# Turning attention probabilities, q and k on VectorE and through DRAM instead of on TensorE, in a single-core attention and FFN kernel

## The reference

```
xn = layernorm(x)
q = xn @ Wq.T   (32 heads of 128)      k, v = xn @ Wk.T, xn @ Wv.T   (8 heads of 128)
q, k = rmsnorm(q, q_norm_w), rmsnorm(k, k_norm_w)     (per head)
scores = q @ k.T / sqrt(128) + slope[head] * (key - query), causal; 4 query heads share one k, v head
attn = softmax(scores);  out = attn @ v;  s = out @ Wo.T
ffn(xn) = (silu(xn @ w_gate.T) * (xn @ w_up.T)) @ w_down.T     (inner width 1376)
result = x + s * silu(ffn(xn))
```

## Time and profile before

| | |
|---|---|
| time of 3 runs, median | 2454.05 us (2453.86 to 2455.95) |
| profiled execution, its own time | 2455.46 us |
| its span, first to last instruction | 2453.7 us |
| busy: PE, PEld, DVE, ACT, POOL | 2422.6, 2070.7, 1693.7, 1236.1, 756.9 us |
| granted TensorE clock, mean | 0.998 |
| DMA traffic | 92.19 MB in 23289 packets, mean 38 GB/s |

### The profile page before, as it was taken

One profiled execution on the slowest core, in us unless ns is written; L12 is line 12 of the kernel. 1 busy time (PEld: TensorE's weight loads), 2 busy tenths in 40 slices (PEclk: granted clock), 3 DMA queues, 4 the chain that ended last, 5 costly groups with the idle time before them and its releaser, 6 DMA issues.

```text
span 2453.7 us, 37432 instructions
## 1 busy us (share of the span) xinstructions
PE 2422.6 (99%) x13232; PEld 2070.7 (84%) x13232; DVE 1693.7 (69%) x3788; ACT 1236.1 (50%) x2548; POOL 756.9 (31%) x2053
## 2 busy tenths in 40 slices
PE   7999999999999999999999999999999999999998
PEld 6888888888888888878888888888888888888887
DVE  7777777777778787823377787777777777777132
ACT  4555554555545555543355555555555545545333
POOL 2323231413233323244522232323232314131443
PEclk9999999999999999999999999999999999999999
DMA  3010000000000000023320101010000000010232
GB/s 130 1 40 4 27 18 27 18 27 18 27 18 27 18 27 18 27 91 125 112 78 1 44 1 44 1 44 1 27 18 26 18 27 18 1 44 14 90 103 103
DMA packets 23289, 92.19 MB, mean 38 GB/s; under 512 B 6592, under 2 KB 6720, under 8 KB 19136
## 3 DMA queue, kind: packets, MB, share of 16 engines
q1 hardware_dynamic: 23104, 89.80, 10.5%
HBM read 85.60 MB, written 4.19 MB: 37 GB/s over the span
## 4 chain that ended last, share of the span: by engine, by line
PE 96%; DVE 2%; ACT 1%; issue 1%; POOL 0%; DMA 0%; DVEq 0%; ACTq 0%; POOLq 0%
PE out_ps L401 17%; PE score_ps L377 16%; PE out_ps L414 14%; PE qkv_ps L351 14%; PE ring_ps L388 10%; PE qkv_ps L352 7%; PE score_ps L504 5%; PE qkv_ps L504 4%; PE ring_ps L520 4%; PE ring_ps L359 2%; PE out_ps L520 1%; PE ring_ps L364 1%; PE score_ps L351 0%; DVE y L997 0%; DVE xT_lo L868 0%
## 5 line engine op out<-in xcount | busy, mean ns | idle before, releaser
L597 ACT ACTIVATE pT_hi<-ring_ps 128x512 fp32r<-128x512 f32 x576 | 344.0, 599 | 509.8 <-PE ring_ps L388 497.2
L818 DVE TENSOR_TENSOR pT_lo<-ring_ps,pT_hi 128x512 fp32r<-128x512 f32 x576 | 396.8, 690 | 90.6 <-ACT pT_hi L597 86.0
L589 ACT ACTIVATE probs<-probs,low_min 128x896 f32<-128x896 f32 (+7 forms) x512 | 395.2, 774 | 50.4 <-DVE low_min L810 50.1
L1016 POOL TENSOR_SCALAR rs_x<-sq_sum 128x5 f32<-128x5 f32 x122 | 24.8, 203 | 1128.1 <-DVE sq_sum L749 1128.1
L388 PE MATMUL ring_ps<-ident,probs 128*128 128x128 f32 x2304 | 345.6, 273 | 0.0
L388 PEld LDWEIGHTS ring_ps<-ident,probs 128*128 128x128 f32 x2304 | 281.7, 140 | 42.1
L810 DVE CUSTOM_DVE_ANT_0 probs<-score_ps,rel_sb,slope 128x512 f32<-128x512 f32 (+5 forms) x504 | 301.7, 599 | 5.7 <-PE score_ps L377 4.3
L377 PE MATMUL score_ps<-kv_hi,qT_hi 128*128 128x320 f32 (+4 forms) x760 | 275.6, 363 | 3.0 <-DVE xT_lo L868 2.0
L401 PE MATMUL out_ps<-pT_hi,kv_hi 128*128 128x512 f32 x576 | 265.8, 461 | 2.9 <-DVE pT_lo L818 2.6
L377 PE MATMUL score_ps<-kv_hi,qT_lo 128*128 128x320 f32 (+4 forms) x760 | 261.0, 343 | 0.0
L377 PE MATMUL score_ps<-kv_lo,qT_hi 128*128 128x320 f32 (+4 forms) x760 | 260.3, 342 | 0.0
(11 more groups left out here) (178 smaller groups left out, 5293.5 us busy)
## 6 DMA issues: line engine op xcount, KB each, us to landing
qkv_raw<-w_ffn_dram SPq DMA_DIRECT2D x44, 768.0 KB, 4.2
qkv_raw<-w_qkv_dram SPq DMA_DIRECT2D x15, 1536.0 KB, 6.9
o_raw<-w_o_dram SPq DMA_DIRECT2D x16, 1024.0 KB, 4.8
o_raw<-x_dram SPq DMA_DIRECT2D x4, 1024.0 KB, 6.7
out_dram<-y SPq DMA_DIRECT2D x16, 256.0 KB, 3.7
probs<-x_dram SPq DMA_DIRECT2D x3, 1024.0 KB, 7.9
qkv_raw<-w_qkv_dram SPq DMA_DIRECT2D x4, 384.0 KB, 6.6
probs<-x_dram SPq DMA_DIRECT2D x2, 512.0 KB, 4.8
```

The source lines that it names most:

```text
L589: act.activation(row, row, ACT.Exp, scale=-1.0, bias=low_min[:, i % 2, h, HEAD_CHUNKS[i] - 1:HEAD_CHUNKS[i]], accum_out=row_sum[:, i % 2, ...
L597: act.activation(pT_hi[:, n % SLOTS, :], ring_ps[:, ring_bank(r), :], ACT.Copy).then_inc(ring_high, 1)
L818: dve.tensor_tensor(out=pT_lo[:, n % SLOTS, :], in0=ring_ps[:, ring_bank(r), :], in1=pT_hi[:, n % SLOTS, :].bitcast(F32), op=ALU.subtract) ...
```

## The change

Probabilities are turned in two stages. VectorE transposes 32x32 blocks in place in `probs` (`turn_blocks`), and SP writes the tile to DRAM and reads it back so that the blocks land in their transposed places: one DMA out, and for each group of up to 4 chunks four DMAs back into `pT`, one for each 32 partitions. q and k of all but the first two tiles of a row go the same way (`scale_qk` with a transpose behind it, `turn_qk` on SP). The division by the row sums is gone from the probabilities; instead the four reciprocals of a tile go through DRAM (`rec_out_at`) and come back broadcast over partitions, and the weighed result is multiplied by them (`scale_att`). `weigh` of tile i - 1 stands as a block behind all scores of step i. `probs` is now one buffer, `pT` is new (two groups of 4 chunks), `pT_hi` keeps 4 slots, and `pT_lo` has 3. Scores have 3 banks instead of 2, and the projections have two pairs of banks. `sum_squares` is gone; ACT squares with an accumulated sum, in five instructions of 128 columns instead of one of 640. `low_att` moves from VectorE to GpSimd, and so do 7 of the 36 `low_probs` of a unit (POOL_LOWS).

The core of the diff follows: the functions of VectorE, the order of VectorE's step, SP, TensorE's step, ACT, GpSimd.

```diff
+                    return
+                dve.tensor_tensor(out=qk[i % 2].rearrange("p (b g n) -> p g b n", b=BLOCKS, g=G + 1),
+                                  in0=acc[:, 0:(G + 1) * P].rearrange("p (g b n) -> p g b n", b=BLOCKS, g=G + 1),
+                                  in1=rq[:, i % 2, :].unsqueeze(2).unsqueeze(3).to_broadcast([P, G + 1, BLOCKS, SQUARE]),
+                                  op=ALU.mult).then_inc(qk_done, 1)
+                dve.wait_ge(qk_done, t)
+                dve.transpose(qk[i % 2], qk[i % 2]).then_inc(qk_turned, 1)
...
+
+            def bias(U, i, k):
 
                 n = SCORE_AT[i] + k
                 h, part = k // HEAD_CHUNKS[i], k % HEAD_CHUNKS[i]
                 lo, hi = [(part + end) * CHUNK_WIDTH[i] for end in range(2)]
                 if k == 0 and i == 0:
...
+            def turn_blocks(U, i, h):
+
+                dve.wait_ge(exped, (tile(U, i) - 1) * G + h + 1)
+                row = by_head[:, h, 0:(i + 1) * BLOCKS, :]
+                dve.transpose(row, row).then_inc(probs_turned, 1)
+
+            def reciprocals(U, i):
+                t = tile(U, i)
+                dve.wait_ge(exped, t * G)
+                if t > 2:
+                    dve.wait_ge(rec_out, (t - 2) * 16)
+                dve.reciprocal(rec[:, i % 2, :], row_sum[:, i % 2, :]).then_inc(rec_done, 1)
+
             def low_probs(U, i, j):
-                r, n = RING_AT[i] + j, TURN_AT[i] + j
-                dve.wait_ge(ring_high, U * RING + r + 1)
-                dve.tensor_tensor(out=pT_lo[:, n % SLOTS, :], in0=ring_ps[:, ring_bank(r), :],
-                                  in1=pT_hi[:, n % SLOTS, :].bitcast(F32), op=ALU.subtract).then_inc(ring_lowd, 1)
-
-            def divide(U, i):
-
-                dve.wait_ge(exped, (U * TILES + i + 1) * G)
-                dve.reciprocal(rec[:, :], row_sum[:, i % 2, :]).then_inc(rec_done, 1)
-                dve.wait_ge(rec_done, U * TILES + i + 1)
-                for h in range(G):
-                    row = probs[i % 2][:, h, 0:(i + 1) * P]
-                    dve.tensor_scalar(row, row, rec[:, h:h + 1], None, ALU.mult).then_inc(divided, 1)
-
...
+            def scale_att(U, i):
+                t = U * TILES + i - 1
+                dve.wait_ge(weighed, (t - 1) // TILES * TURNS + TURN_AT[(t - 1) % TILES + 1])
+                dve.wait_ge(rec_back[t % 2], ((t - 1) // 2 + 1) * 16)
+                scaled = att[i % 2][:, :].rearrange("p (g a n) -> p g a n", g=G, a=BLOCKS)
+                dve.tensor_tensor(out=scaled, in0=out_ps[:, :].rearrange("p (a g n) -> p g a n", g=G, a=BLOCKS), in1=scaled,
+                                  op=ALU.mult).then_inc(att_scaled, 1)
 
             def add_y(U, i, copy):
...
+                    for k in range(sooner, chunks):
+                        bias(U, i, k)
+                        h, part = divmod(k, HEAD_CHUNKS[i])
+                        if k - sooner < len(sooner_lows):
+                            low_probs(V, p, sooner_lows[k - sooner])
+                        if part == HEAD_CHUNKS[i] - 1 and h >= 2:
+                            turn_blocks(U, i, h - 2)
+                    for j in sooner_lows[max(0, chunks - sooner):]:
+                        low_probs(V, p, j)
...
+                                low_x(0, t)
+                    if i < TILES:
+                        turn_blocks(U, i, G - 2)
+                        turn_blocks(U, i, G - 1)
+                        reciprocals(U, i)
+                    for j in lows:
+                        low_probs(V, p, j)
...
+                m, slot = turned_before(t), t % 2
+                alone(qk_turned, m + 1)
+                if m >= 2:
+                    alone(qk_back[m % 2], m // 2 * BLOCKS * 16)
+                sp.dma_start(qk_out_at[slot], qk[i % 2]).then_inc(qk_out, 16)
+                alone(qk_out, (m + 1) * 16)
+                there = qk_out_at[slot].rearrange("(a r) (b m) -> b r a m", a=BLOCKS, b=BLOCKS)
+                for k in range(BLOCKS):
+                    sp.dma_start(qk[i % 2][k * SQUARE:(k + 1) * SQUARE, :].rearrange("r (a m) -> r a m", a=BLOCKS),
+                                 there[k]).then_inc(qk_back[m % 2], 16)
...
+            def turn_probs(U, i):
+
+                t = tile(U, i)
+                slot = t % 2
+                alone(probs_turned, t * G)
...
+                sp.dma_start(turned_out[slot, 0:i + 1].rearrange("j p m -> p j m"), by_chunk[:, 0:i + 1, :]
+                             ).then_inc(probs_out, 16)
+                alone(rec_done, t)
+                if t > 2:
+                    alone(rec_back[slot], (t - 1) // 2 * 16)
+                sp.dma_start(rec_out_at[slot].rearrange("g p -> p g"), rec[:, i % 2, :], allow_slow_non_contiguous=True).then_inc(rec_out, 16)
+                alone(probs_out, t * 16)
+                for part in range(GROUPS_IN[i]):
+                    lo, hi = part * GROUP, min((part + 1) * GROUP, i + 1)
+                    group = U * GROUPS + GROUP_AT[i] + part
+                    if group >= 2:
+                        done = chunks_to_group(group - 2)
+                        alone(low_by_dve, done // TURNS * DVE_LOW_AT[TURNS] + DVE_LOW_AT[done % TURNS])
+                        alone(low_by_pool, done // TURNS * POOL_LOW_AT[TURNS] + POOL_LOW_AT[done % TURNS])
+                    there = turned_out[slot, lo:hi].rearrange("j (a r) (b m) -> b r (j a) m", a=BLOCKS, b=BLOCKS)
+                    for k in range(BLOCKS):
+                        at = group % 2 * GROUP
+                        sp.dma_start(pT[k * SQUARE:(k + 1) * SQUARE, at:at + hi - lo, :]
+                                     .rearrange("r j (a m) -> r (j a) m", a=BLOCKS), there[k]).then_inc(probs_back[group % 2], 16)
+                alone(rec_out, t * 16)
+                if t > 2:
+                    alone(att_split, t - 2)
+                sp.dma_start(att[i % 2][:, :], rec_out_at[slot:slot + 1].rearrange("a g p -> a (g p)").to_broadcast([P, G * P])
+                             ).then_inc(rec_back[slot], 16)
+
...
-                ring_free(U, r, first)
-                for h in range(G):
-                    if j == 0:
-                        pe.wait_ge(divided, (U * TILES + i - 1) * G + h + 1)
-                    tr = pe.transpose(ring_ps[:, ring_bank(r), h * P:(h + 1) * P],
-                                      probs[p % 2][:, h, j * P:(j + 1) * P], ident[:, :])
-                tr.then_inc(ring_full, 1)
-
-            def weigh(U, i, j, turns, first):
-
...
             def step(U, i, first, last):
-                ahead = not (last and i >= TILES - 1)
+                if not (last and i >= TILES - 2):
+                    project(U + (i + 2) // TILES, (i + 2) % TILES, first and i + 2 < TILES)
...
+                for k in range(sooner):
+                    scores(U, i, k, first)
+                if not (first and i < 2):
+                    out_project(U, i)
+                for k in range(sooner, chunks):
+                    scores(U, i, k, first)
...
+            def squares(U, i, first):
+                t, acc = tile(U, i), acc_of(i, first)
                 act.wait_ge(projected, t)
-                if not first:
-                    act.wait_ge(summed, t - 1)
-                act.activation(qk_sq, acc[:, 0:(G + 1) * P], ACT.Square).then_inc(squared, 1)
-
-            def stage_v(acc, i, t, early):
-                if not early:
-                    act.wait_ge(v_split, t - VBUFS)
-                act.activation(v_nat[:, i % VBUFS, :], acc[:, BANK + P:BANK + KV], ACT.Copy).then_inc(v_staged, 1)
-
...
-            def high_probs(U, i, j, first):
-                r, n = RING_AT[i] + j, TURN_AT[i] + j
-                act.wait_ge(ring_full, U * RING + r + 1)
-                if not (first and n < SLOTS):
-                    act.wait_ge(weighed, U * TURNS + n - SLOTS + 1)
-                act.activation(pT_hi[:, n % SLOTS, :], ring_ps[:, ring_bank(r), :], ACT.Copy).then_inc(ring_high, 1)
+            def high_probs(U, i, j):
...
+                group = U * GROUPS + GROUP_AT[i] + j // GROUP
+                act.wait_ge(probs_back[group % 2], (group // 2 + 1) * BLOCKS * 16)
+                if U * TURNS + n >= HIGH_SLOTS:
+                    act.wait_ge(weighed, U * TURNS + n - HIGH_SLOTS + 1)
...
+                    highs = [] if i > TILES or first and i == 0 else list(range(p + 1))
+                    if i == 0:
+                        for j in highs[:HIGH_SLOTS]:
+                            high_probs(V, p, j)
+                        highs = highs[HIGH_SLOTS:]
+                    if not (last and i >= TILES - 2):
+                        squares(U + (i + 2) // TILES, (i + 2) % TILES, first and i + 2 < TILES)
...
+                        high_o(U, 1, not first)
+                    if i:
+                        for j in highs[:HIGH_SLOTS]:
+                            high_probs(V, p, j)
+                        highs = highs[HIGH_SLOTS:]
+                    if i < TILES:
```

(15 more changed lines are left out.)

642 lines of the change are left out of this document (319 added, 323 removed).

## The result

The changed kernel takes 4060.89 us (median of 4 runs, 4054.24 to 4065.72) against 2455.0 us before: a ratio of 1.654 (95% interval 1.651 to 1.657). The forecast was 2950 us, with a range of 2560 to 3320. The direction was right; the size was missed by 1111 us, 8.7 us in each of 128 steps.

What follows compares the result with a forecast made beforehand. The kernel before was taken as bound by TensorE, the changed one by a loop through DRAM: eight steps make 158.8 us a unit, 16 units plus 409 us for start, FFN and row ends give 2950 us, range 2560 to 3320.

Steps and rivals of the forecast that it cites:

- unit: Stretch of eight steps from one load of the slopes to the next; forecast to last 158.8 us, 16 of them.
- R: Round trip of a tile's probabilities out to DRAM and back: 8.1 to 15.0 us for 2 to 8 chunks.
- V: VectorE's work in a step from first low part to last transpose: 4.6 to 10.9 us for tiles 2 to 7.
- the sentence on the reciprocals: The reciprocals' 4-byte packets on the DMA queue: 0 to 1.5 us a step, 0 to 190 us in all, taken as 0.
- The loop: Once a step, tile i's transposes wait for tile i-1's way back: R + 0.6 + V, 13.3 to 25.8 us; chance 50%.
- The signs that the prediction named for it: In the profile after, tile 7's store issue to its first group's landing takes 12 to 16 us.
- Its bounds 0.78 and 1.55: Lower and upper price in us of each 256 KB chunk on the way back; the middle, 1.16, was taken.
- The q and k trip: q and k through DRAM, issued early in a step, wanted over 10 us later; claimed hidden behind the loop.
- Rival 1: The round trip is hidden and only the second path binds: 130 us a unit, 2493 us; chance 12%.
- the second path: Low parts, weighing, projection, Wo, first score and bias, then V, one behind another; sets step 1, 15.7 us.
- Rival 3: TensorE's clock falls after idling, projection and Wo take 12.5 instead of 6.9 us: 3160 us; chance 20%.
- Rival 4: The DMA queue binds, if 512-byte packets cost three times large ones: 190 us a unit, 3450 us; chance 8%.

Runs made afterwards that it cites:

- experiment 5: The change with the reciprocals padded and turned on VectorE, leaving as 16 packets of 128 bytes instead of 512 of 4; 3192.39 us, ratio 1.300.
- experiment 8: As experiment 5, with next slopes loaded right behind tile 7's store and weights in quarters and halves behind the ways back; 3134.32 us, ratio 1.278.
- experiment 6: The kernel before, with single transfers added behind its last store, each waited for, to price them; the 512 packets of 4 bytes took 8.2 us.
- experiment 7: As experiment 5, but ACT does all exponentials ahead of the previous tile's high parts and VectorE all transposes ahead of low parts; 3182.37 us, ratio 1.296.
- experiment 4: The change with each DMA back reading packets of 2 KB instead of 512 bytes into 32 partitions, blocks left unturned; 3873.28 us, ratio 1.578.

## Why the prediction was wrong

**Where the 1111 us went.** 869 us are the 4-byte packets (experiment 5 against the change), 58 the loads at the turn of a unit (experiment 8), and 3134 - 2950 = 184 us are left. Of the last the unit shows the place. SP's issues of `turned_out<-probs` in experiment 8, the first and the last of nine from tile 7 to the next tile 7; the table has the distances from one to the next:

```profile
697.80 0.38 SPq L309 DMA_DIRECT2D turned_out<-probs  x1
...
867.02 0.38 SPq L309 DMA_DIRECT2D turned_out<-probs  x1
```

| step | 0 | 1 | 2 | 3 | 4 | 5 | 6 | 7 | unit |
|---|---|---|---|---|---|---|---|---|---|
| forecast | 19.9 | 15.7 | 13.3 | 16.6 | 20.4 | 23.0 | 24.1 | 25.8 | 158.8 |
| experiment 8 | 22.8 | 16.7 | 16.4 | 16.8 | 22.3 | 22.6 | 24.9 | 26.9 | 169.2 |

With the small packets gone, steps 3 and 5 to 7 are within 1.1 us of the forecast; steps 0, 2 and 4 are 2 to 3 us longer. The unit is 10.4 us longer, 16 x 10.4 = 166 of the 184 us. (The next unit is 167.6; there step 2 takes 14.5.)

None of it is the round trip. From the issue of the store to ACT's first high part it is 9.5, 11.9, 12.1, 13.6, 13.7 and 14.5 us for n = 3 to 8, where R was 10.0, 11.9, 12.7, 13.5, 14.3 and 15.0. Step 0 has SP's row in front of its store (experiment 8). Step 2 has GpSimd, by the chain of waits (start us, us, what):

```profile
737.66 2.34 POOL o_lo L1122
...
741.24 1.24 POOL attT_lo L1162
742.52 4.61 PE out_ps L493 x12
```

GpSimd splits the new Wo there, and `attT_lo` stands behind it; TensorE waits 2.89 us for it, and the projection by Wo then takes 4.6 us at a granted clock of 0.64, against 3.0 at 1.00 in the next unit. The forecast had called `low_att` on GpSimd hidden. In step 4 it is V: 9.4 us instead of 7.9, with one low part of 1.77 us where the others take 0.69 (GpSimd takes its own low part at that moment) and scores at a granted clock of 0.50.

**The step that failed** is the sentence on the reciprocals: "Between nothing and 1.5 us a step, 0 to 190 us in all; I take 0 because the queue is idle then." Measured, 8.2 us for the transfer alone, and 869/128 = 6.8 us a step. With this part mended the forecast's sum is 242 us short, and the kernel of experiment 5, at 3192 us, lies inside its range. Two things were wrong in the sentence. The upper end, 1.5 us, was a guess at 2 KB; the nearest row of the trace was that of a small load, and no row had more than one packet to a partition of such a size. I should have looked at the packets: 512 of 4 bytes in one DMA, of a kind that no row prices, so its upper bound is far away. And the reason, an idle queue, was wrong twice: in an idle queue the transfer takes 8.2 us all the same (experiment 6), and L311 is issued 0.6 us behind the store, so it never has an idle queue; it lands either with the store or ahead of the way back. The loop has no slack, so both come to the same. The Trainium skill would have helped: DMA: Bandwidth & Descriptors, in the part Measured of its section Bandwidth, puts the floor of a small transfer down to its packets, at about 10.5 ns each. By that 512 packets are 5.4 us, an estimate. The trace has 8.2 us to the landing, but not as time of the packets: their records end 1.3 us behind the issue. The page names another direction and another way of issue than here.

**R otherwise.** The round trip was right where it was priced: 6.9 us for a group back against 6.7, and 1.75 MB out in 6.7 against 7.2. The signs that the prediction named for it hold in experiment 8, with 14.5 us for tile 7 (12 to 16 expected). Its bounds 0.78 and 1.55 hold it; the middle was the right choice, as the nearest row alone was not.

**V and the transposes** were right within 0.3 us in the change's steps of tiles 5 and 6 and 3% in the price of a column; step 4 of experiment 8 is 1.5 us over.

**The q and k trip.** "Hidden" was right in the steps of large tiles and wrong in the small ones behind the turn of a unit: `qk_out_at<-natural` is 6% of the chain of the change. Weights of 1.5 MB stood ahead of it in the queue and the slopes behind 2 MB on their way back; with both moved, it still holds up the store of tile 0.

**Rival 1 and the second path.** The mechanism is real and the price was 326 us too low: the path goes through ACT (squares, the copy of v, the weights) and GpSimd (Wo, `attT_lo`), and not only through TensorE and VectorE. With the trip free a unit is still 151 us, against 169 with it, so the loop alone can give back 18 us a unit at the most. The order of experiment 7 opens the loop and lengthens the second path, and the two nearly cancel (10 us).

**Rival 3, the clock.** It fell as described: around one step of tile 5 the windows of the change read as follows (us, busy us of PE, PEld, DVE, ACT, POOL, then the granted clock, DMA share, GB/s).

```profile
1058.00:1066.00 8.00, 1.02 (x5) 0.47 (x3) 0.63 (x2) 0.41 (x1) 7.00 (x17) 0.79 0.58 107
...
1071.00:1075.00 4.00, 4.00 (x12) 3.30 (x12) 3.96 (x11) 2.55 (x5) 0.00 (x0) 0.50 0.33 82
...
1118.00:1124.00 6.00, 6.00 (x32) 5.10 (x31) 1.79 (x3) 1.57 (x11) 2.22 (x7) 1.00 0.14 21
```

TensorE had idled 10.59 us before 1070.65, and then ran at 0.50 of 2.4 GHz, which is the 1.2 GHz level. The rule of the Trainium skill cited in the prediction (TensorE: Matmul & The Clock Gate, Part 1: The HAM clock gate) agrees: an idle engine comes back at half rate. In that step this fell mostly on scores that VectorE paced. The last window is of the next step, and most of its projection lies there at the full level, where the rival had the projection at half. But the clock was not free: the two weighings and the first matmuls ahead of that window, from 1113.7 to 1117.2, ran at the half level, and in the same step half-rate scores stand in the chain of waits:

```profile
1103.21 2.71 PE score_ps L452 x6
```

Six such matmuls take 1.2 us at the full level. V of that step still came out within 0.3 us of the forecast. So the clock is a part of what is left over, some 1.5 us of the chain in this step by these rows, an estimate; its whole price was not measured.

**Rival 4, the DMA queue as the bound,** was wrong as put: the queue's engines are busy 48% of the span of the change and 57% in experiment 7, where DMA is 7% of the chain. That small packets can cost far more than their bytes was right; the rival put it on the packets of 512 bytes, and it belonged to those of 4.

No version of this change that was run beats the kernel before. The best, experiment 8, is 28% slower; and with its whole trip through DRAM for nothing it is 15% slower still.

## What to carry to other kernels

Look at the packets of each added DMA, not only at its bytes: 2 KB in packets of one element took longer here than 1 MB in packets of 512 bytes, and transfers issued beside it were late too. Where no row prices such a transfer, price it alone before forecasting with it. Turn such data on the chip first, so that it leaves in rows. And before trusting that a path is the bound, lead the next one through every engine's row, those called slack too: a second path of nearly the same length takes what the first gives back.

## What the runs showed of the hardware

- 2 KB to DRAM: 512 packets of 4 bytes 8.2 us, 128 packets of 16 bytes 1.5 to 2.3 us, 16 packets of 128 bytes 2.2 us with four issues. The packets themselves are through 1.3 us behind the issue; the landing comes 6.9 us later. With 1 MB out ahead of them both land after 10.9 to 12.9 us (4.45 us for the 1 MB alone), and 1 MB back behind them lands 14.7 to 15.9 us after their issue (6.9 us alone).
- An issue can block its engine. In the step at 1085.52, SP took 12.92 us for eight issues, one of them 8.63 us; in experiment 6, where every group is waited for, an issue of such a load takes 0.32 to 0.51 us. A backlog so shows as time of SP in the chain (SPq 10% after, 5% in experiment 8).
- 1 MB from DRAM by four DMAs: into 32 partitions each 6.7 to 6.9 us in packets of 512 bytes and 6.5 to 6.7 in packets of 2 KB, over all 128 partitions in packets of 512 bytes 5.8 to 6.0 us.
- Not settled: why larger packets on the way back (experiment 4) gave 188 us beside the 4-byte packets, when by itself the form is at most 0.3 us cheaper a group (192 groups, under 60 us); why stores and loads are late by turns in the change; and what of the 4-byte packets, number, size or addresses, delays the landing.
